# Low-rank matrices and the copied sums prepared early in the last wd product, and one eviction ahead of block 3's low parts

## What is computed

```
s = silu(x @ wg.T); the half of s with the smallest |s| is set to 0, per token
x = layernorm(x + (s * (x @ wu.T)) @ wd.T)              # 1024 -> 2752 -> 1024
def q(x, w, A, B): return x @ tile(w, (1, 4)).T + 0.5 * (x @ A.T @ B.T)   # rank 2
x = layernorm(x + q(silu(q(x, w1, a1, b1)) * q(x, w3, a3, b3), w2, a2, b2))
```

## Time and profile before

| | us |
|---|---|
| median of 3 runs | 1863.69 |
| lowest and highest | 1860.75, 1864.17 |
| the profiled execution | 1862.13 |
| its span in the trace | 1860.2 |
| TensorE busy | 1840.7 (99% of the span) |
| VectorE busy | 1468.3 (79%) |
| GpSimd busy | 957.5 (51%) |
| ScalarE busy | 719.9 (39%) |

### The profile page before, as it was taken

How to read it: one execution, slowest core, us unless ns; L and a number is a source line. 1 busy time by engine, 2 the same in 40 slices (tenths; PEclk the granted TensorE clock), 3 DMA queues, 4 the chain that set the end, 5 groups by cost and what they waited for, 6 DMA issues and landing times.

```text
span 1860.2 us, 23661 instructions
## 1 busy us (share of the span) xinstructions
PE 1840.7 (99%) x8584; PEld 1533.3 (82%) x8584; DVE 1468.3 (79%) x2077; ACT 719.9 (39%) x1177; POOL 957.5 (51%) x705
## 2 busy tenths in 40 slices
PE   9999999999999999999999999999999999999998
PEld 8898888978889789888888988888887777777776
DVE  2138899988988695898878768988588899889973
ACT  4346544474233434722343365233323232223312
POOL 5446697546655854465466545554568232023410
PEclk9999999999999999999999999999999999999999
DMA  4333248734377743334786334366953112312212
GB/s 147 93 101 97 86 147 236 204 98 142 97 232 227 226 129 104 113 128 131 236 256 195 93 107 142 98 212 193 278 179 141 35 46 101 135 62 77 102 46 91
DMA packets 123511, 258.65 MB, mean 139 GB/s; under 512 B 13860, under 2 KB 35876, under 8 KB 120168
## 3 DMA queue, kind: packets, MB, share of 16 engines
q1 hardware_dynamic: 118784, 240.34, 41.7%
q10 hardware_dynamic: 4608, 16.78, 2.2%
HBM read 215.65 MB, written 41.42 MB: 138 GB/s over the span
## 4 chain that ended last, share of the span: by engine, by line
PE 83%; POOL 5%; DVE 5%; ACT 4%; DMA 3%; issue 1%; SPq 0%; POOLq 0%; DVEq 0%; ACTq 0%
PE banks L1596 28%; PE banks L1597 27%; PE banks L1598 27%; POOL wl L659 3%; ACT junka L815 2%; DMA w_in_place<-in_wg 2%; DVE junkx L1083 1%; PE banks L1788 1%; POOL xTl L659 1%; ACT wh L766 1%; POOL w2l L659 1%; DMA w_in_place<-in_wd 0%; DVE qa L1125 0%; POOL w L688 0%; PE banks L1801 0%
## 5 line engine op out<-in xcount | busy, mean ns | idle before, releaser
L659 POOL TENSOR_TENSOR wl<-w_in_place,wh 128x512 fp32r<-128x512 f32 (+2 forms) x552 | 751.8, 1367 | 573.1 <-ACT wh L766 571.9
L766 ACT CAST wh<-w_in_place 128x512 fp32r<-128x512 f32 (+2 forms) x560 | 329.0, 589 | 724.2 <-DMA w_in_place<-in_wg 281.2
L1596 PE MATMUL banks<-wh,xTh 128*128 128x512 f32 (+2 forms) x1536 | 565.0, 368 | 5.4 <-POOL wl L659 5.3
L1598 PE MATMUL banks<-wh,xTl 128*128 128x512 f32 (+2 forms) x1536 | 563.2, 367 | 0.0
L1597 PE MATMUL banks<-wl,xTh 128*128 128x512 f32 (+2 forms) x1536 | 563.1, 367 | 0.0
L1596 PEld LDWEIGHTS banks<-wh,xTh 128*128 128x128 f32 x1536 | 288.3, 188 | 51.4 <-POOL wl L659 9.6
L1598 PEld LDWEIGHTS banks<-wh,xTl 128*128 128x128 f32 x1536 | 288.3, 188 | 40.1
L1597 PEld LDWEIGHTS banks<-wl,xTh 128*128 128x128 f32 x1536 | 288.3, 188 | 39.6
L1596 PE MATMUL banks<-wh,hTh 128*128 128x512 f32 x672 | 263.2, 392 | 2.2 <-POOL wl L659 2.1
L1598 PE MATMUL banks<-wh,hTl 128*128 128x512 f32 x672 | 262.2, 390 | 0.0
L1597 PE MATMUL banks<-wl,hTh 128*128 128x512 f32 x672 | 262.2, 390 | 0.0
(11 more groups left out here) (151 smaller groups left out, 2194.9 us busy)
## 6 DMA issues: line engine op xcount, KB each, us to landing
w_in_place<-in_wd SPq DMA_DIRECT2D x176, 256.0 KB, 2.7
w_in_place<-in_wg SPq DMA_DIRECT2D x128, 256.0 KB, 3.0
w_in_place<-in_wu SPq DMA_DIRECT2D x128, 256.0 KB, 2.7
turning<-squares SPq DMA_DIRECT2D x16, 1024.0 KB, 5.1
landed<-turning SPq DMA_DIRECT2D x64, 256.0 KB, 3.9
w_in_place<-in_w SPq DMA_DIRECT2D x54, 256.0 KB, 2.9
x_in_place<-in_xT SPq DMA_DIRECT2D x32, 256.0 KB, 5.2
y<-in_xtok SPq DMA_DIRECT2D x4, 2048.0 KB, 8.5
```

Source lines behind the costliest of these rows:

```text
L659: nc.gpsimd.tensor_tensor(lo, landed, hi.bitcast(F32), ALU.subtract).then_inc(done, 1)
L766: nc.scalar.copy(hi, piece).then_inc(hi_done, 1)
L1596: nc.tensor.matmul(dst, ah, bh, start=start, stop=False)
L1598: return nc.tensor.matmul(dst, al, bh, start=False, stop=stop)
```

## The change

- The rows of a1 and a3 for the last wd product are loaded to a place of their own, arow_last, which lies over chunks 2 to 5 of w2h and no longer over b13's memory. The dots of tokens(2, t) read them there.
- The clearing of braw moves from after take_up(3) into it, behind the last transposes of the squares. The loads of b1 and b3 stand at d = 7 to 12 instead of 12 to 17.
- ScalarE scales braw into b13 at d = 13 and there waits only for the loads. Its wait for tok_done is at d = 34, ahead of the cast of w2's fifth piece, the first that would overwrite arow_last.
- On VectorE the fills of split_b and split_x, the clearing of rep, the twelve copies for blocks 0 and 1 and the two instructions on b13 come ahead of the low parts of set 5 and of the tokens. The fill of sel stays behind the tokens.
- In second(1) the eviction of block 1's tile 3 comes ahead of block 3's low parts and low-rank input, and the statistics of tile 2 behind them.

```diff
@@ memory @@
+        arow_last = sb("arow_last", [P, 2 * R, H], F32, 4, offset=at["w2h"] + 2 * H * 4)
@@ load_a_row @@
-                sp.dma_start(v[:, c, I - H:I], arow[:, c, :]).then_inc(a_in, 16)
+                sp.dma_start(v[:, c, I - H:I] if b < NB else arow_last[:, c, :], arow[:, c, :]).then_inc(a_in, 16)
@@ SyncE, last wd product @@
-                if 12 <= d < 18:
-                    load_b((d - 12) // 2, d % 2)
+                if 7 <= d < 13:
+                    load_b((d - 7) // 2, (d - 7) % 2)
@@ ScalarE, last wd product @@
-                if d == 32:
+                if d == ND - NW2 + 2:
                     act.wait_ge(tok_done, 3 * NT)
+                if d == 13:
                     act.wait_ge(b_in, 16 * 12)
                     nc.scalar.mul(b13[0:LX, :], braw[0:LX, :], LORA).then_inc(b_ready, 1)
@@ VectorE, tokens @@
-                        step(V.scalar_tensor_tensor(out=junkx[:, :], in0=x[:, :], scalar=1.0, in1=v[:, R * w + r, I - H:I],
+                        a = v[:, R * w + r, I - H:I] if b < 2 else arow_last[:, R * w + r, :]
+                        step(V.scalar_tensor_tensor(out=junkx[:, :], in0=x[:, :], scalar=1.0, in1=a,
@@ VectorE, take_up @@
                     turn(b, j)
+                    if b == NB - 1 and j == NJ - 1:
+                        st.done()
+                        V.memset(braw[:, :], 0.0).then_inc(b_zero, 1)
@@ VectorE, behind the last take_up @@
-            V.memset(braw[:, :], 0.0).then_inc(b_zero, 1)
-            turned(NB - 1, NJ - 1)
-            for t in range(NT):
-                tokens(NB - 2, t)
             for part, new, old, n in ((split_b, (LORA, -1.0), (0.0, 1.0), 2 * R), (split_x, (1.0, -1.0), (0.0, 1.0), R)):
...
-            dve.wait_ge(xf_out, 16 * NT * (NB - 1))
-            fill(sel[:, :, :], 0.0)
-            for r in range(R):
-                V.memset(sel[:, r, T2 + r:T2 + r + 1], LORA).then_inc(sel_ready, 1)
-
@@ behind the copies for blocks 0 and 1 @@
-            dve.wait_ge(small_in, 16)
             dve.wait_ge(b_ready, 1)
             step(V.tensor_scalar(braw[0:LX, :], braw[0:LX, :], split_b[0:LX, 0:1], None, ALU.mult))
             st.done()
             V.scalar_tensor_tensor(out=b13[0:LX, :], in0=b13[0:LX, :].bitcast(F32), scalar=split_b[0:LX, 1:2],
                                    in1=braw[0:LX, :], op0=ALU.mult, op1=ALU.add).then_inc(b_ready, 1)
+            turned(NB - 1, NJ - 1)
+            for t in range(NT):
+                tokens(NB - 2, t)
+            dve.wait_ge(small_in, 16)
+            dve.wait_ge(xf_out, 16 * NT * (NB - 1))
+            fill(sel[:, :, :], 0.0)
+            for r in range(R):
+                V.memset(sel[:, r, T2 + r:T2 + r + 1], LORA).then_inc(sel_ready, 1)
@@ VectorE, second(1) @@
                     sums(1)
-                    sums(2)
+                    take_out(1, 3)
                     for k in range(KQ):
                         low_xf(3, k)
                     low_rank_x(3)
-                    take_out(1, 3)
+                    sums(2)
                     sums(3)
```

## The result

The changed kernel takes 1870.18 us (median; 1868.31 to 1873.77) and the kernel before, beside it on the same chip, 1862.33: a ratio of 1.0046, with a 95% interval of 1.0032 to 1.0060. It is slower by some 8 us. Forecast was 1860.4, within 1857.9 to 1864.5, so the forecast and its range were wrong, and a slower kernel had been given a chance of 0.06. The profiled execution took 1873.77 us, with a span of 1871.8 against 1860.2 before.

What follows compares the result with a forecast made beforehand. TensorE, busy for 99% of the span, bounds the kernel, so only its standing or slow time can be won. -3.95 + 2.2 - 1.5 = -3.25 us, against the median of 1863.69 giving 1860.4, range 1857.9 to 1864.5.

Steps and rivals of the forecast that it cites:

- The gain at d=33 and d=42: Last wd product: TensorE's waits of 0.27 and 1.96 us and 1.72 us of low clock go, 3.95 us won.
- The copies: VectorE's idle stretch before set 5's low parts: the twelve copies fit there and take 2 to 6 us.
- rival 3: Last wd product: copies take 14.9 us, b13 begins at 1354.1, token 1 is 8.4 late: +4.65, 1868.3 us; chance 0.07.
- as in time, or late by 1: Last wd product: braw's loads, issued five d (13.6 us) sooner, have 8 us to land and come in time or 1 late.
- ScalarE's scaling at 1347.9: Last wd product: d=13's second cast ends at 1345.4, the scaling adds 2.51, so b13 can start at 1347.9.
- d=15 instead of d=14, 1.4 us: Last wd product: b13's second instruction delays GpSimd's low part for d=14; TensorE stands 1.4 us, counted within the 2.2.
- set 5's low parts: VectorE behind b13: four low parts, 0.5 us each alone and 1.34 beside GpSimd, take 2 to 5 us.
- The tokens, +2.2 at d=26: Last wd product: token 1's sum ends later, SyncE holds back d=26's load, TensorE loses 2.2 us, between 0.5 and 3.
- The clock: Last wd product: the loss by d=26 is divided, neither gap reaches 1.8 us, so the 1.7 us clock fall is not counted.
- The eviction, -1.5: Near 1650, second half of the last stage: TensorE's 1.42 us wait and the restart go, 1.5 us won, bounds 1.2 and 1.6.

Runs made afterwards that it cites:

- lighter pairs: The kernel before with eight sums into acc (p = 4, first half of the second stage) left out: 1860.98 us, ratio 0.9992.
- late loads: Changed kernel with b1 and b3 loads at d = 12 to 17, scaling at d = 22, b13's VectorE instructions behind or among the token sums: 0.9991 each at first.
- the eight pieces: Changed kernel with b13's second VectorE instruction cut into eight of 344 columns, each waiting for the one before: 1869.20 us, ratio 1.0039.
- b13 between the sums again: Second measurement: changed kernel, loads at d = 12 to 17, scaling at d = 22, b13's instructions behind token 1's and token 2's sums: 1858.90 us, 0.9980.

## Why the prediction failed, step by step

- **The gain at d=33 and d=42, -3.95: right in its mechanism, too large on the average.** Neither wait is in the profile after. (The 19.07 us that the prediction puts between d=26 and d=33 are the regular time of 84 matmuls; the rows give 19.34, and the 0.27 is right.) But the product's length says 3.2 (above). The forecast took the one profile as the rule: the wait at d=42 is 1.80 us there, and 1.08, 1.33 and 1.85 with the eviction alone, with early loads and with lighter pairs, and behind these three the clock stayed up, so the 1.72 for it was no fixed cost.
- **The copies: right that they fit.** Forecast 2 to 6 us, they took 1.02, twelve in a row, and ended at 1345.9. So fast is luck: GpSimd had nothing to do then, since wd's piece was late. With late loads they took 2.14, 3.27 and 3.28 us. What rival 3 held against them didn't occur.
- **braw's loads "as in time, or late by 1": this step failed first.** It asked whether braw lands in time, not who lands later for it. braw itself held nothing up: the scaling follows the late casts without a wait of its own. The last sentence of the prediction named the case, a load of wd late near d=11, and left it without a price or a chance. It costs 1.07 + 4.08 + 1.52 = 6.7 us of TensorE. A view that bore on it was to be had: the DMA share of 0.96 to 1.06 from 1330 to 1345, in the kernel before.
- **ScalarE's scaling at 1347.9: failed by that.** It ended at 1358.24, behind d=13's cast, and b13 at 1363.9 instead of 1352.3 to 1354.7.
- **d=15 instead of d=14, 1.4 us: the term was mis-sized.** The lock was seen, and its place nearly. But the price was one instruction's length. The low part at 1361.04 waited for the 2.9 us left of b13's second, for set 5's four low parts (1.9) and for a dot (1.2) and then had its own 1.1: 7.05 us, and TensorE lost 4.14 + 1.62 = 5.8. The sum that set 5's low parts would take "2 to 5 us" beside GpSimd had assumed that the two engines take turns; the four took 1.95, because GpSimd got no turn. The Trainium skill (SBUF — State Buffer, "SBUF: two separate sides") gives the pair of ports to whichever of the two starts first, for the whole instruction. The long low part agrees with that. Here VectorE had its next instruction ready each time and went first five times in a row; where it waited for a semaphore in between, as between the eight pieces, GpSimd got in.
- **The tokens, +2.2 at d=26: not tested by the changed kernel.** The sums started at 1365.76, not 1356.8, and token 1's ended at 1386.9, ten us later than before, but TensorE was late already. The chain itself is real, as the pieces showed at d=23.
- **The clock, "neither gap reaches 1.8, and I take no fall": the reading of two cases doesn't hold.** Waits of 1.82 to 2.54 us left the clock up five times, and one of 1.61 brought it down (last section). It didn't decide anything here, since the long waits, 3.92 and 3.98 us, came elsewhere.
- **The eviction, -1.5: right.** 2 us alone (with an interval that reaches 1.0001), and 1.6 in the profile after. As forecast, xsl isn't moved: it starts 0.03 us after the first pair's first matmul, as before. Timelines of TensorE and VectorE after, against the earlier trace rows:

```profile
1659.86 0.48 PE L1600 MATMUL banks<-xsh,w13h 128*128 128x512 f32 x1
...
1658.83 0.69 DVE L1515 TENSOR_TENSOR y<-banks,y 128x512 f32<-128x512 f32 x1 [0.24 <-PE banks L1602]
1659.89 1.29 DVE L1423 TENSOR_TENSOR xsl<-banks,xsh 128x512 fp32r<-128x512 f32 x2 [0.37 <-ACT xsh L952]
```

- **Rival 3** had the sign and nearly the sum, 1868.3, and its shape: b13 held back to 1358, as it had reckoned 1354. But its cause was another, and so was where TensorE paid: at d=11 and d=15, not at d=26.

With the two terms put in, -3.95 + 6.7 + 5.8 - 1.5 = +7.05 us; measured are 6.7 without the race in the pairs, and 7.85 with it. That this comes so near is partly luck, since each term is of one profile. By the product's mean lengths it is 8.4 less 1.6 for the eviction, 6.8.

## What to carry to other kernels

Where a load is moved earlier, look at how busy the DMA engines are in the stretch that it enters, and whose loads there have little slack: here 258 KB, in transfers of two partitions each, held up four pieces of 256 KB by 3.2 to 8.6 us. Whether it is the two partitions that make them dear wasn't tested. And where VectorE gets a run of instructions with two inputs in SBUF and no wait between them, cost what GpSimd has due by the length of the whole run, not of one instruction. A profile shows one way in which a race falls; where two versions differ by a few us, take out the race first.

## What the runs showed of the hardware

Waits of TensorE of the same length did and didn't bring its clock down. The granted clock over 3.5 us behind a wait of 1.80 us in the kernel before was 0.54, and behind 1.85 us at the same place of the same code with lighter pairs 1.00; at the end of the pairs it stayed at 1.00 behind 1.82, 2.42 and 2.45 us and fell to 0.54 behind 1.61, to 0.63 behind 1.80, to 0.56 behind 2.45 and to 0.64 behind 2.52. Of all thirteen waits of 1.59 to 2.54 us from the last wd product on it fell behind seven. Behind all eight waits over 3.5 us it fell, to 0.50 to 0.71. So a price for "the clock falls" on a wait of 1.6 to 2.6 us is a chance, not a sum. The stretch behind 1.85 us, lighter pairs in the kernel before:

```profile
1428.59:1432.09 3.50, 3.50 (x15) 2.92 (x16) 3.50 (x5) 0.00 (x0) 3.50 (x3) 1.00 0.00 0
```

behind 1.82 us, b13 between the sums again:

```profile
1570.82:1574.32 3.50, 3.50 (x15) 2.89 (x16) 3.46 (x5) 1.32 (x2) 1.50 (x1) 1.00 0.97 407
```

and behind 2.45 us at the same place, the eviction alone:

```profile
1577.45:1580.95 3.50, 3.50 (x9) 2.78 (x10) 3.46 (x5) 1.32 (x2) 1.49 (x1) 0.56 1.01 426
```
